# Six attention layers: the row maximum is subtracted on VectorE instead of by a TensorE product

## The reference

```python
q = q * cos * scale + rotate_half(q) * sin * scale      # after l2norm
k = k * cos * inv + rotate_half(k) * sin * inv
sim = jnp.einsum('bhwie,bhwje->bhwij', bq, bk2) * QK_SCALE   # QK_SCALE = 8, window 32, 64 keys
sim = jnp.where(mask, -jnp.finfo(sim.dtype).max, sim)
attn = jax.nn.softmax(sim, -1)
out = jnp.einsum('bhwij,bhwje->bhwie', attn, bv2)
```

## Time and profile before

| | us |
|---|---|
| median of three runs | 5128.53 |
| lowest, highest | 5125.22, 5132.47 |
| the profiled execution | 5129.49 |
| its span, first to last instruction | 5127.7 |
| busy: PE, DVE, ACT, POOL | 4725.2, 3840.9, 3167.3, 1796.5 |

### The profile page before, as it was taken

How to read it: one execution, slowest core, us unless ns; L and a number is a source line. 1 busy time by engine, 2 the same in 40 slices (tenths; PEclk the granted TensorE clock), 3 DMA queues, 4 the chain that set the end, 5 groups by cost and what they waited for, 6 DMA issues and landing times. The chain is left out here.

```text
span 5127.7 us, 120607 instructions
## 1 busy us (share of the span) xinstructions
PE 4725.2 (92%) x45392; PEld 3555.8 (69%) x45392; DVE 3840.9 (75%) x6774; ACT 3167.3 (62%) x5142; POOL 1796.5 (35%) x966
## 2 busy tenths in 40 slices
PE   6888887699999999999999999999999999869999
PEld 2333332588877887778877888777877787648788
DVE  5665664788888888888888888888888888656554
ACT  4666655467666666667766766676766676523333
POOL 0000000555544555555545555455545555200000
PEclk9999999899999999999999999999999999979999
DMA  0000000222212222222222222222222222110000
GB/s 24 7 6 6 12 4 5 81 62 57 55 48 79 56 59 57 68 60 56 58 53 78 56 56 59 69 61 55 57 54 78 55 56 55 40 44 9 8 6 4
DMA packets 133931, 232.27 MB, mean 45 GB/s; under 512 B 29208, under 2 KB 33952, under 8 KB 132128
## 3 DMA queue, kind: packets, MB, share of 16 engines
q1 hardware_dynamic: 133408, 225.16, 16.8%
HBM read 32.11 MB, written 4.19 MB: 7 GB/s over the span
## 5 line engine op out<-in xcount | busy, mean ns | idle before, releaser
L660 POOL TENSOR_TENSOR qk_rotated<-qk_rotated,rotary_sines 128x1024 f32<-128x1024 f32 x384 | 914.1, 2381 | 1391.5 <-DVE rotary_sines L748 1391.5
L671 POOL TENSOR_TENSOR qk_rotated<-qk_rotated,rnorm 128x1024 f32<-128x1024 f32 x384 | 747.4, 1947 | 314.9 <-DVE rnorm L814 307.5
L756 DVE TENSOR_REDUCE qk_sumsq<-qk_squared 128x16 f32<-128x1024 f32 x384 | 467.5, 1217 | 299.9 <-ACT qk_squared L502 299.8
L221 PE MATMUL ps_proj<-qkv_w_hi,x_shifted_hi 128*128 128x512 f32 x1152 | 492.5, 427 | 47.5 <-DVE qkv_w_lo L716 24.1
L509 ACT ACTIVATE q_t<-ps_qk_t 128x512 f32<-128x512 f32 x384 | 229.4, 597 | 459.3 <-PE ps_qk_t L277 459.3
L738 DVE TENSOR_TENSOR qk_rotated<-ps_proj,rotary_scaled 128x1024 f32<-128x1024 f32 x384 | 466.8, 1216 | 4.4 <-ACT qk_squared L502 4.4
L748 DVE TENSOR_TENSOR rotary_sines<-ps_proj,rotary_scaled 128x1024 f32<-128x1024 f32 x384 | 466.6, 1215 | 0.2 <-POOL qk_rotated L660 0.2
L523 ACT ACTIVATE k_t_by_head<-ps_qk_t 64x512 f32<-64x512 f32 x768 | 451.8, 588 | 12.2 <-PE ps_qk_t L286 2.9
L222 PE MATMUL ps_proj<-qkv_w_lo,x_shifted_hi 128*128 128x512 f32 x1152 | 457.0, 397 | 0.0
L223 PE MATMUL ps_proj<-qkv_w_hi,x_shifted_lo 128*128 128x512 f32 x1152 | 457.0, 397 | 0.0
L502 ACT ACTIVATE qk_squared<-ps_proj 128x1024 f32<-128x1024 f32 x384 | 392.2, 1021 | 70.6 <-DVE qk_sumsq L756 52.6
(11 more groups left out here) (239 smaller groups left out, 10680.6 us busy)
## 6 DMA issues: line engine op xcount, KB each, us to landing
v_by_window<-v_tokens SPq DMA_DIRECT2D x1152, 128.0 KB, 2.4
v_by_window<-v_tokens SPq DMA_DIRECT2D x384, 64.0 KB, 2.1
v_by_window<-v_by_window SPq DMA_DIRECT2D x192, 64.0 KB, 2.0
qkv_w_raw<-in_layer_qk_dram SPq DMA_DIRECT2D x7, 1664.0 KB, 7.8
layer_w<-in_layer_w_dram SPq DMA_DIRECT2D x6, 580.5 KB, 3.9
layer_w<-in_layer_w_dram SPq DMA_DIRECT2D x6, 512.0 KB, 3.5
f_x<-in_x_dram SPq DMA_DIRECT2D x8, 256.0 KB, 2.8
f_x_tail<-in_x_dram SPq DMA_DIRECT2D x8, 256.0 KB, 3.3
```

What stands on the lines that cost most here:

```text
L221: mm(out, hi, HI[:, o:o + 512], start=True, stop=False)
L660: tt(u, u, TB[:], ALU.add).then_inc(added, 1)
L671: tt(u, u, r.unsqueeze(3).broadcast_to((P, 2, 8, DH)), ALU.mult).then_inc(scaled, 1)
L756: nc.vector.reduce_sum(SS[:, 16 * i:16 * i + 16], SQ[:].rearrange("p (h e) -> p h e", e=DH), AX).then_inc(sumsq, 1)
```

## The change

The product `shift` on PE goes, with its four places in the turn. `row_max` on DVE now writes the maximum itself (not negated), and DVE issues a second instruction right behind it: it waits for the maximum, reads S and the broadcast maximum, subtracts, and writes the difference into the probabilities' buffer E. ACT's exp then reads E and writes E in place. The bank S is free for the next group's scores when the subtraction is done (the semaphore `shifted`), where it was free after the exp (`exped`). The two waits that protect E's buffer (`pt_mm`, `esum`) move from ACT to DVE.

```diff
@@ score (PE)
-                after(pe, exped, g.n)
+                after(pe, shifted, g.n)
@@ PE
-            def shift(g):
-
-                if g.live:
-                    pe.wait_ge(nmax, g.n + 1)
-                    mm(S[:].rearrange("p (a e) -> p a e", e=DH), IDR[:], NMX[:].unsqueeze(2).broadcast_to((P, 8, DH)), start=False, stop=True,
-                       skip_group_check=True).then_inc(shifted, 1)
@@ turn (PE), the same at groups 1, 2 and 3
                 q_t(gt[0])
-                shift(gs[0])
@@ exps (ACT)
                     act.wait_ge(shifted, g.n + 1)
-                    after(act, pt_mm, g.n - 1)
-                    after(act, esum, g.n - 1)
-                    a(E[:, g.k % 2, :], S[:], ACT.Exp, scale=8.0).then_inc(exped, 1)
+                    a(E[:, g.k % 2, :], E[:, g.k % 2, :], ACT.Exp, scale=8.0).then_inc(exped, 1)
@@ row_max (DVE)
                     dve.wait_ge(scores, g.n + 1)
-                    nc.vector.tensor_reduce(NMX[:], S[:].rearrange("p (a e) -> p a e", e=DH), AX, ALU.max, negate=True).then_inc(nmax, 1)
+                    nc.vector.tensor_reduce(MX[:], S[:].rearrange("p (a e) -> p a e", e=DH), AX, ALU.max).then_inc(nmax, 1)
+                    dve.wait_ge(nmax, g.n + 1)
+                    after(dve, pt_mm, g.n - 1)
+                    after(dve, esum, g.n - 1)
+                    tt(E[:, g.k % 2, :].rearrange("p (a e) -> p a e", e=DH), S[:].rearrange("p (a e) -> p a e", e=DH),
+                       MX[:].unsqueeze(2).broadcast_to((P, 8, DH)), ALU.subtract).then_inc(shifted, 1)
```

More of the change, by code:

```diff
@@ L102, in layers_phase @@
         GG = sb("gate", [P, HCH, N])
-        NMX = sb("neg_max", [P, 8], F32R)
+        MX = sb("row_max", [P, 8])
         SM, RS = sb("row_sum", [P, 8]), sb("row_rsum", [P, 8])
@@ L437, in turn @@
                 q_t(gt[1])
-                shift(gs[1])
                 q1(n1)
@@ L451, in turn @@
                 q_t(gt[2])
-                shift(gs[2])
                 hidden2(h, e)
@@ L465, in turn @@
                 q_t(gt[3])
-                shift(gs[3])
                 if j == B + 1 and more(layer):
```

## The result

The changed kernel takes 5346.6 us (median of four runs, 5345.2 to 5351.0), the kernel before 5126.9 in the same comparison. The ratio is 1.0429, interval 1.0411 to 1.0447: slower, by 220 us where 190 were forecast, and inside the stated range.

The account below looks back on a forecast made before the run. It took a ring of waits over DVE and ACT, hardly PE, as the bound: 1.94 us a turn times 96 is 186 us, plus 3 for the exp, on 5129.5 gives 5319 us. Own range 5290 to 5345, stated range 5262 to 5380.

Parts of the forecast that it names:

- The ring: One turn's dependences close over some 13 us on ACT, 19 us on DVE and only 3 us on PE.
- The price of one subtraction: On DVE behind each row maximum: 0.72 us more per group, as 0.72 + 0.60 = 1.32 us replaces 0.60.
- Groups 3 and 0: Between row_max3 and row_max1 DVE waits only for itself, so both subtractions count in full: 1.44 us a turn.
- Group 1: Later sines of piece 1 delay hidden01 and the probabilities' transposes; ACT's copy starts 0.50 us later, 0.22 us falling into slack.
- the shift of group 2 that goes: Removed product on PE, 0.32 us each: only group 1's is in the ring; gain put at nothing.
- Group 2: Subtraction hidden by DVE's 1.93 us idle before the fourth sum of squares, 1.43 left: costs nothing.
- The sum: 0.50 + 0.72 + 0.72 = 1.94 us a turn over 96 turns is 186 us, plus 3 for the exp.
- a term that the prediction had named (up to 9 us): Turns between two layers, where DVE splits the next weights without idle time: up to 0.94 us in each of ten.
- a clock still at 1.00: PE's granted clock in the profile after would stay 1.00, its higher level, though its share falls to 88 to 90%.
- PE as the bound: Rival: sparing PE products and waits shortens every turn, together 224 us, to 4905 us; chance 4%.
- DVE as the bound throughout: Rival: all four subtractions count, 2.88 us a turn, 276 us, giving 5406 us; chance 14%, including part of it.
- hold the subtraction up: Rival: POOL's scaling delays group 0's subtraction 1.13 us a turn, 108 us more, giving 5427 us; chance 3%.

Follow-up runs that it names:

- e6: Kernel before, with the subtraction on DVE in place 2 (the prediction's group 2) alone: ratio 1.0004, regular turn 35.91 us.
- e1: Kernel before, with the subtraction on DVE in place 0 (the prediction's group 0) alone: ratio 1.0178, 5222 us, regular turn 36.74 us.
- e2: Kernel before, with the subtraction on DVE in place 3 (the prediction's group 3) alone: ratio 1.0195, 5233 us, regular turn 36.71 us.
- e4: Changed kernel, with the earlier group's output scaling put between maximum and subtraction on DVE: ratio to before 1.0340, 5305 us, regular turn 37.67 us.
- e8: Changed kernel, with PE transposing place 1's probabilities ahead of hidden01 instead of behind it: ratio to before 1.0351, 5309 us, regular turn 37.57 us.
- e7: Changed kernel, with four unread 512-column products a turn added on PE where it waits ahead of v1: ratio to before 1.0387, 5326.8 us.

## Why the prediction was right

**The ring.** The main step, that the turn is a ring over DVE and ACT with little of PE in it, held: a spared TensorE product of 0.30 us bought 0.10 us in a regular turn (e6), and DVE time put into the ring counted.

**The price of one subtraction.** 0.72 us from start to start of what is around it: measured 0.73 and 0.70 alone (e1, e2), and its parts 0.60 and 0.12 by e4.

**Groups 3 and 0.** 1.44 forecast; 0.70 + 0.73 = 1.43 apart.

**Group 1.** 0.50 forecast, 0.73 alone. In the company of group 2 the two cost 0.62. I had not seen the second path, by hidden2 and the third gate. The forecast for the changed kernel came out well because that path is relieved just there by the shift of group 2 that goes, which the prediction had put at nothing. In the changed kernel e8 took 0.41 of the 0.50 away on the path that was forecast; so this step was near in its size, incomplete in its reason, and the size owes something to luck.

**Group 2.** Nothing forecast, -0.10 measured, and its cover is in the trace: 1.52 us left of 1.93 (1.43 forecast). The 0.19 us of idle time that the subtraction has ahead of it here was not forecast and is covered too.

**The sum.** A regular turn +1.94 forecast with 0.03 for the exp (630 ns from SBUF after, 596 before), +1.97 measured. By the places apart 0.73 + 0.70 + 0.62 = 2.05; the 0.08 us too much are not explained. That the sum comes out to a hundredth is in part luck: places 1 and 2 cost 0.12 more than was forecast when they alone are changed, and the four together cost 0.08 less than their parts.

**What the 190 missed of the 220.** The regular turns make 187 us. TensorE's clock makes 20, by e7: 14.6 in the 17 long turns, and 5 in ten turns at the changes of layer. These ten turns, in which DVE also splits the next weights, took 2.9 us more each than before, and 2.4 in e7 with fewer falls of the clock, where a regular turn took 1.97: another 4 us, a term that the prediction had named (up to 9 us) and left out of the sum. The remaining 9 us, in the loop's other turns at a change of layer and at both ends, I have not taken apart. The prediction was wrong in one sign that it named, a clock still at 1.00; it took that from the earlier trace rows, from a kernel whose longest regular pause of PE was 0.74 us. The Trainium skill (TensorE: Matmul & The Clock Gate, on the clock gate) says that the granted clock follows how busy PE has been recently; the trace agrees so far as the falls come behind two pauses, of 0.64 and 1.17 us, and go when e7 fills the longer one; it shows too that in most turns the clock stays at 1.00 behind the same two pauses.

**The rivals.** PE as the bound is excluded by e6, which took a product of 0.30 us out of each turn and made the regular turn 0.10 us shorter. DVE as the bound throughout is excluded by e6 too, which put 0.69 us of DVE's work into that same turn. POOL did not hold the subtraction up: those of group 0 ran beside POOL's scaling (2410.52 in POOL's 2409.57 to 2411.65) and took 0.69 us like all others, 690 to 694 ns over all 384. The Trainium skill's rule of the shared port (SBUF — State Buffer, the two separate sides of SBUF), read by its words, was right to clear an operation with one operand in PSUM. The trace agrees with it in the experiments also: `rstd_diag`, with two operands in SBUF, was held there for 2.0 to 2.1 us, in six kernels in which it started behind POOL. POOL did hold DVE up, then, 35 times, at another instruction than the one that the rival named, and in none of the turns of the changed kernel.

## What to carry to other kernels

Before moving work from the busiest engine to another, follow one period around its ring of waits and price the work at the place where it goes: here the same subtraction cost 0.7 us in three places of a turn and nothing in the fourth. An engine that is 96% busy may be outside the ring. And when PE loses work without the period getting shorter, price its new pauses at the lower clock as well. Last, a regular turn is not the whole time: e6 came out unchanged because five long turns took back what its regular turns had won.

## What the runs showed of the hardware that I had not expected

PE pauses of 0.64 and 1.17 us, out_t0 and v1, were followed in about one turn in five by some three microseconds at the lower clock, and 0.9 us of PE products in the longer pause were enough to stop that (e7). What selects the turn is open: the regular turns have the same two pauses.

With the subtraction in one or two places only, the long turns are of another kind. They begin with a small DVE instruction that takes 2.0 to 2.1 us instead of 0.42, because it starts 0.1 to 0.2 us behind POOL's scaling and not 0.11 us ahead of it. A fifth of a microsecond on one engine so costs 1.9 us in the turn, and more where the clock falls behind it.
